# Message sums of a graph layer: rows stationary in 32 bit and a ring of sixteen slots, in a GNN and expert kernel on one core

## The reference

```python
def gcn_conv(x, W, b, src, dst, n_nodes):
    loop = jnp.arange(n_nodes)
    s = jnp.concatenate([src, loop])
    d = jnp.concatenate([dst, loop])
    ...
    norm = dinv[s] * dinv[d]
    xw = x @ W
    msg = xw[s] * norm[:, None]
    out = jax.ops.segment_sum(msg, d, num_segments=n_nodes)
    return out + b

out = gcn_conv(x, W1, b1, src, dst, N_NODES)
out = jax.nn.relu(batch_norm(out, gamma1, beta1))
out = gcn_conv(out, W2, b2, src, dst, N_NODES)
out = batch_norm(out, gamma2, beta2)
out = jax.nn.relu(out + identity)
```

## Time and profile before

| | us |
|---|---|
| median of three timed runs | 6407.3 |
| the profiled execution, its own time | 6353.42 |
| span of the profile | 6351.4 |
| TensorE busy in the span | 4421.4 (70%) |
| GpSimd busy | 3436.0 (54%) |
| VectorE busy | 1942.5 (31%) |
| ScalarE busy | 1190.9 (19%) |
| mean granted clock of TensorE | 0.709 |

### The profile page before, as it was taken

One profiled execution on the slowest core, in us unless ns is written; L12 is line 12 of the kernel. 1 busy time (PEld: TensorE's weight loads), 2 busy tenths in 40 slices (PEclk: granted clock), 3 DMA queues, 4 the chain that ended last, 5 costly groups with the idle time before them and its releaser, 6 DMA issues. The chain is left out here.

```text
span 6351.4 us, 77947 instructions
## 1 busy us (share of the span) xinstructions
PE 4421.4 (70%) x14346; PEld 2126.4 (33%) x14347; DVE 1942.5 (31%) x6975; ACT 1190.9 (19%) x2762; POOL 3436.0 (54%) x3661
## 2 busy tenths in 40 slices
PE   4567776676667766667766766666666665569999
PEld 3322222222222222232222222222222224448888
DVE  9411121211111112251122212212212216656665
ACT  5100000000000000020000000000000006635554
POOL 0266666666666666556666666666666662221111
PEclk5566666676666766766667676677677776679999
DMA  3643333333333333343333333333333332321111
GB/s 99 216 114 90 89 89 89 91 89 89 89 90 88 92 89 89 84 118 90 90 88 89 90 89 90 90 89 90 89 89 89 90 85 72 106 73 50 48 49 45
DMA packets 265568, 568.06 MB, mean 89 GB/s; under 512 B 67392, under 2 KB 139938, under 8 KB 265507
## 3 DMA queue, kind: packets, MB, share of 16 engines
q0 software_dynamic: 171264, 466.46, 25.5%
q1 hardware_dynamic: 94242, 100.94, 5.6%
HBM read 507.06 MB, written 60.09 MB: 89 GB/s over the span
## 5 line engine op out<-in xcount | busy, mean ns | idle before, releaser
L593 POOL DMA_INDIRECT ring<-messages,idx_stage x3328 | 3150.7, 947 | 1816.4 <-issue 875.5
L1591 PE MATMUL ps<-ring,onehot_mem 128*64 128x256 f32 x6656 | 2834.0, 547 | 1128.0 <-DMA ring<-messages,idx_stage 575.0
L1591 PEld LDWEIGHTS ps<-ring,onehot_mem 128*64 128x64 f32 x6656 | 933.4, 180 | 2665.9 <-DMA ring<-messages,idx_stage 1732.3
L1088 DVE TENSOR_TENSOR acc<-acc,ps 128x128 f32 x832 | 240.0, 288 | 3740.8 <-remote 2119.9
L727 ACT ACTIVATE win_rows<-ps 64x256 f32<-64x256 f32 x832 | 313.0, 377 | 2187.1 <-PE ps L1591 968.6
L1077 DVE TENSOR_SCALAR onehot_mem<-iota_bf,tables 128x64 f32<-128x64 bf16 x3344 | 647.4, 269 | 185.2 <-issue 135.8
L1488 PE MATMUL ps<-ident,win_rows 64*128 64x64 f32 x1664 | 340.0, 297 | 425.2 <-ACT win_rows L727 337.7
L1488 PEld LDWEIGHTS ps<-ident,win_rows 64*128 64x128 f32 x1664 | 207.9, 175 | 926.9 <-issue 926.9
L716 ACT ACTIVATE idx_stage<-tables 128x8 int32 (+1 forms) x420 | 87.0, 207 | 2292.0 <-PE ps L1591 982.5
L1796 PE MATMUL ps<-acc 128*128 128x256 f32 x2048 | 467.2, 380 | 0.8 <-ACT acc L890 0.8
L652 POOL DMA_INDIRECT out_dram<-acc x128 | 127.3, 995 | 600.7 <-DVE acc L1441 420.1
(11 more groups left out here) (250 smaller groups left out, 2213.4 us busy)
## 6 DMA issues: line engine op xcount, KB each, us to landing
ring<-messages,idx_stage POOLq DMA_INDIRECT x3328
rows_mem<-in_x_dram SPq DMA_DIRECT2D x62, 448.0 KB, 4.7
acc<-routed_rows SPq DMA_DIRECT2D x64, 264.0 KB
messages<-dinvT SPq DMA_DIRECT2D x28, 448.0 KB, 6.3
dinvT<-in_x_dram SPq DMA_DIRECT2D x22, 448.0 KB, 4.0
dinvT<-dinv_row SPq DMA_DIRECT2D x28, 224.0 KB
messages<-ring SPq DMA_DIRECT2D x14, 448.0 KB, 3.2
messages<-rows_mem SPq DMA_DIRECT2D x14, 448.0 KB, 3.2
```

Source lines behind the costliest of these rows:

```text
L593: pool.indirect_dma_start(out=slots[:, s, :], out_offset=None, in_=t_dram[layer], in_offset=bass.IndirectOffsetOnAxis(ap=idx_stage[:, u, s ...
L1088: dve.tensor_tensor(sums(w, WIN), sums(w, WIN), ps[:, 2 + u, 0:KH * WIN].rearrange("p (k w) -> p k w", k=KH), ALU.add).then_inc(ev_fast, 1)
L1591: pe.matmul(ps[0:WIN, u, 0:D], onehot[:, u, j, 0:WIN], slots[:, s, :], start=j == 0, stop=j == CPG - 1).then_inc(chunks_used, 1)
```

## The change

- The gathered rows, 32-bit, become the stationary operand. For each half k of the features and each chunk j, one matmul has 128 features of the slot stationary and moves the 64 columns of the one-hot. The group's sum appears as features by nodes in one bank, both halves side by side. Copy by ScalarE, turn by TensorE, `win_rows` and two semaphores go.
- VectorE adds straight from the bank. Four banks are used in turn, and four sets of one-hots (`DEEP` = 4), made four groups ahead.
- The ring has sixteen slots, eight in `ring` and eight in `rows_mem`. A group of four gathers counts up one semaphore (`got[q]`, 64 for a group), and TensorE waits once for all four.
- `chunks_used` is raised once a group, by four, on the last matmul. GpSimd waits for it once a group.
- The indices are still staged by eights (`STAGE`) in two buffers.

```diff
-SLOTS = 8
+SLOTS = 16
+DEEP = SLOTS // CPG
+STAGE = 8
...
-        slots = ring[:, 0:SLOTS * D].rearrange("p (s f) -> p s f", s=SLOTS)
-        onehot = onehot_mem[:, 0:2 * CPG * WIN].rearrange("p (u j w) -> p u j w", u=2, j=CPG)
+        slots = [mem[:, n * D:(n + 1) * D] for mem in (ring, rows_mem) for n in range(SLOTS // 2)]
+        onehot = onehot_mem[:, :].rearrange("p (u j w) -> p u j w", u=DEEP, j=CPG)
...
-                    for s in range(SLOTS):
-                        wait(pool, chunks_used, c0 + s - SLOTS + 1 + done)
+                    for h in range(STAGE // CPG):
+                        q = u * (STAGE // CPG) + h
+                        wait(pool, chunks_used, i * SLOTS + (q + 1) * CPG - SLOTS + done)
                         hold(pool)
-                        pool.indirect_dma_start(
-                            out=slots[:, s, :], out_offset=None, in_=t_dram[layer],
-                            in_offset=bass.IndirectOffsetOnAxis(ap=idx_stage[:, u, s:s + 1], axis=0),
-                        ).then_inc(got[s], 16)
+                        for j in range(CPG):
+                            n = h * CPG + j
+                            pool.indirect_dma_start(
+                                out=slots[q * CPG + j], out_offset=None, in_=t_dram[layer],
+                                in_offset=bass.IndirectOffsetOnAxis(ap=idx_stage[:, u, n:n + 1], axis=0),
+                            ).then_inc(got[q], 16)
...
-                    wait(act, chunks_used, (i - 1) * (2 * SLOTS) + u * SLOTS + SLOTS + done)
+                    wait(act, chunks_used, (i - 1) * SLOTS + (u + 1) * STAGE + done)
...
-                def keep_window(g, u):
-                    act.wait_ge(chunks_used, (g + 1) * CPG + done)
-                    wait(act, win_turned, g - 1 + layer * NG if not isinstance(g, int) or g > 1 else 0)
-                    hold(act)
-                    act.activation(win_rows[:, u, :], ps[0:WIN, u, 0:D], ACT.Copy).then_inc(win_kept, 1)
...
                 def fast(g, u):
                     dve.wait_ge(chunks_used, (g + 1) * CPG + run * GATHERS)
                     hold(dve)
-                    make_onehot(g + 2, u)
+                    make_onehot(g + DEEP, u)
                     w = dve.value_load(wrow[0:1, bass.ds(g, 1)], min_val=0, max_val=WMAX)
-                    dve.wait_ge(win_turned, g + 1 + run * NG)
...
-                def fast(i, q):
-                    g, u = i * 4 + q, q % 2
-                    pe.wait_ge(oh_fast, g + 1 + run * (NG + 2))
-                    for j in range(CPG):
-                        s = (q * CPG + j) % SLOTS
-                        landed(s, i * 2 + (q * CPG + j) // SLOTS)
-                        pe.matmul(ps[0:WIN, u, 0:D], onehot[:, u, j, 0:WIN], slots[:, s, :],
-                                  start=j == 0, stop=j == CPG - 1).then_inc(chunks_used, 1)
-                    if not isinstance(g, int) or g > 0:
-                        turn_window(g - 1, 1 - u)
+                def fast(i, q):
+                    g = i * DEEP + q
+                    pe.wait_ge(oh_fast, g + 1 + run * (NG + DEEP))
+                    wait(pe, ev_fast, g - DEEP + 1 + run * NG if not isinstance(g, int) or g >= DEEP else 0)
+                    landed(q, i)
+                    for k in range(KH):
+                        for j in range(CPG):
+                            last = pe.matmul(ps[:, q, k * WIN:(k + 1) * WIN], slots[q * CPG + j][:, k * P:(k + 1) * P],
+                                             onehot[:, q, j, :], start=j == 0, stop=j == CPG - 1)
+                    last.then_inc(chunks_used, CPG)
```

More of the change, by code:

```diff
@@ L127, in gnn_moe @@
         srcT = tables[:, TG * CPG:2 * TG * CPG]
-        ring = sb("ring", [P, max(SLOTS * D, 2 * BPC * (D + 8) + KH * CH)])
+        ring = sb("ring", [P, max(SLOTS // 2 * D, 2 * BPC * (D + 8) + KH * CH)])
         onehot_mem = sb("onehot_mem", [P, CPG * GWIN])
@@ L136, in gnn_moe @@
         iota_bf = sb("iota_bf", [P, GWIN], BF16)
-        idx_stage = sb("idx_stage", [P, 2, SLOTS], I32)
+        idx_stage = sb("idx_stage", [P, 2, STAGE], I32)
         relk = sb("relk", [P, CPG])
@@ L334, in gnn_moe @@
         GATHERS = NG * CPG
-        STAGES = GATHERS // SLOTS + 2
+        STAGES = GATHERS // STAGE + 2
         L1, L2 = 0, 1
@@ L721, in stages @@
                         stage(i, u)
-                def keep_window(g, u):
-                    act.wait_ge(chunks_used, (g + 1) * CPG + done)
-                    wait(act, win_turned, g - 1 + layer * NG if not isinstance(g, int) or g > 1 else 0)
-                    hold(act)
-                    act.activation(win_rows[:, u, :], ps[0:WIN, u, 0:D], ACT.Copy).then_inc(win_kept, 1)
                 def fours(i):
-                    for q in range(4):
-                        if q % 2:
-                            stage(i + 1, q // 2)
-                        keep_window(i * 4 + q, q % 2)
+                    stages(i + 1)
                 def add_bias(t):
@@ L933, in _ @@
             dve.tensor_copy(iota_bf[:, :], iota_i).then_inc(iota_bf_ready, 1)
-            dve.memset(ring[:, SLOTS * D:], 0.0)
+            dve.memset(ring[:, SLOTS // 2 * D:], 0.0)
             dve.wait_ge(edges_in, 32)
@@ L1131, in fours @@
                     for q in range(4):
-                        fast(i * 4 + q, q % 2)
+                        fast(i * DEEP + q, q)
                 def stride_end(g):
@@ L1140, in aggregate @@
                 with dve.If(bad == 0):
-                    for u in range(2):
+                    for u in range(DEEP):
                         make_onehot(u, u)
@@ L1569, in product @@
                     for k in range(KH):
-                        last = pe.matmul(ps[:, k, 0:GWIN], slots[:, s, k * P:(k + 1) * P], onehot_gen[:, j, :],
+                        last = pe.matmul(ps[:, k, 0:GWIN], slots[s][:, k * P:(k + 1) * P], onehot_gen[:, j, :],
                                          start=j == 0, stop=j == CPG - 1)
                     return last
-                def landed(s, use):
-                    pe.wait_ge(got[s], 16 * (use + done // SLOTS + 1))
-                def turn_window(g, u):
-                    pe.wait_ge(win_kept, g + 1 + run * NG)
-                    wait(pe, ev_fast, g - 1 + run * NG if not isinstance(g, int) or g > 1 else 0)
-                    hold(pe)
-                    for k in range(KH):
-                        last = turn(ps[:, 2 + u, k * WIN:(k + 1) * WIN], win_rows[:, u, k * P:(k + 1) * P])
-                    last.then_inc(win_turned, 1)
@@ L1585, in fast, with landed @@
[L1585 to L1594 removed]
+                def landed(q, use):
+                    pe.wait_ge(got[q], 16 * CPG * (use + done // SLOTS + 1))
@@ L1596, in general @@
                 def general(i, u):
-                    g = i * 2 + u
-                    for j in range(CPG):
-                        landed(u * CPG + j, i)
+                    g = i * DEEP + u
+                    landed(u, i)
                     hold(pe)
@@ L1630, in fours @@
                 def fours(i):
-                    for q in range(4):
+                    for q in range(DEEP):
                         fast(i, q)
@@ L1653, in aggregate @@
                 with pe.Else():
-                    with pe.Fori(0, NG // 2) as i:
-                        for u in range(2):
+                    with pe.Fori(0, NG // DEEP) as i:
+                        for u in range(DEEP):
                             general(i, u)
```

20 lines of the change are left out of this document (8 added, 12 removed).

## The result

The changed kernel takes 6489.06 us (median of 4 runs, 6484.09 to 6491.45) against 6406.89 us (6396.28 to 6411.36): ratio 1.013, 95% interval 1.0112 to 1.0147. It is 1.3% slower. The forecast was 5796 us in a range of 5680 to 6230: wrong in sign, and outside the range. The profiled run took 6484.09 us.

The account below looks back on a forecast made before the run. No engine was full; TensorE's late signals stalled GpSimd's gathers in the two aggregations. From 6353.4 us, minus 711 of stalls, plus 100 remaining, gives 5742; with 53.9 from profiled run to median, 5796 us, range 5680 to 6230.

Parts of the forecast that it names:

- The pace: Gathers in both aggregations: GpSimd starts one every 1.25 us by itself, so a layer takes 2079.7 us.
- TensorE's size: Products of a group: 16 records in 3.65 us slow or 1.9 fast, under the 5.0 us of four gathers.
- the fast cases: Remaining stalls with all products at the fast clock level: 178 us, weighted 0.36 against 410 us slow.
- VectorE locking GpSimd out: Rival in the aggregations: VectorE's 887 us of one-hots and sums hold up gathers, 6683 us; chance 0.03.
- The loop of the index copy: Index staging before every second group: 11.0 us slow, 9.25 fast, within 15.0, covering lateness of 4.0 or 5.75 us.
- What is left of the stalls: Aggregations: 832 measured latenesses played through the new waiting rules leave 326 us; cut to three quarters, 100 us.
- cover too short: Rival in the aggregations: lateness grows with what is queued; 6326 us, within 6022 to 6390; chance 0.12.
- the slower rival: Whole-group hand-over: steady lateness above 7.4 us makes the index loop longer than before; at 8.6, 6657 us; chance 0.10.
- 711 us of stalls: Both aggregations before the change: 353.8 + 357.5 us beyond GpSimd's own gather pace, all a deeper ring can bring.
- nothing left: Lower end of the forecast case: no stalls remain in the aggregations, 5696 us.
- the carried median: Whole kernel: the runs' median lies 53.9 us above the profiled run, added to the forecast.

Follow-up runs that it names:

- The run of 6333.68 us: The changed kernel with row numbers copied once the gathers reading the old ones have landed, not once TensorE used the rows; 6333.68 us, 0.9983 of the kernel before.
- by chunk: The changed kernel with TensorE waiting for and signalling each gather separately, and row numbers copied once their gathers landed; 6374.84 us, 1.004 of the kernel before.

## Why the prediction was wrong

- **The pace** held: 0.95 us busy and 0.30 idle, 1.25 from gather to gather, whatever surrounds it. A layer without stalls takes 2082.6 us where 2079.7 were worked out.
- **TensorE's size** held: 13312 records, waits for landings, 16 records in 3.65 us at the slow level and 1.90 at the fast one. The clock fell to 0.53, so it was at the slow level nearly throughout: 637 of 832 groups took 3.6 to 3.75 us and only 38 under 2.5, which took the fast cases out of the sum. One of those few:

```profile
1512.59 1.90 PE L1576 MATMUL ps<-onehot_mem,ring 128*128 128x64 f32 x16
```

- **VectorE locking GpSimd out** did not happen: 949 ns median with 3360 one-hots beside.
- **The loop of the index copy** was right in place: the stall sits before an even group, ended by the index copy. In size it was 0.5 us short. I had read 0.6 us from copy to gather off, where the gather at 1550.45 waited for a slot too ("remote"); behind a copy that is really waited for, the gather starts 1.06 us after it (middle half 1.05 to 1.07, 223 pauses), and as much in the run with signals 5.0 us late. So the loop is 11.5 us and covers 3.5, not 4.0, and 5.0 + 11.5 + 7.6 gives the 24.1 us of a round.
- **The step that failed is "What is left of the stalls".** I took 832 measured latenesses as a property of the signals, cut them to three quarters and played them through a longer cover: 100 us left. Measured: 854 us, 143 more than before. The run of 6333.68 us shows why: the lateness follows the cover. It is 7.7 us where 3.5 are covered and 12.7 to 14.2 where 9.8 are, and GpSimd pauses either way, the first signal coming 3.8 to 4.0 us after its last gather began. That the pause is what lets the signal go is argued from this timing; no run with a longer pause written in tested it. In the earlier trace rows the late signals did come together, after a long unbroken run of gathers. The "cover too short" rival said so and I gave it 0.12, and "it would have to be so always", with which I put off the slower rival, is exactly what a held signal does.
- **Why slower and not the same.** Where signals are late, the changed kernel and the one with the copy after landing both pause about once in 16 gathers whatever they cover (the one before once in 11, for less; by chunk once in 13). In the changed kernel the resuming gather also waits for ScalarE: signal 1542.78, copy 1542.93, gather 1543.99; and the product that has to end first is a whole group's. With the copy after landing the ratio is 0.9983 and not 1.013. That difference of 1.5%, some 95 us, is what the index copy costs where signals are late (compared through the kernel before, since the two ran on different chips); the rest of the change is worth 0.2% there.
- **The starting point.** 711 us of stalls are there in one measurement and not in another. On one without, the changed kernel takes 5593 us: the case "nothing left" had 5696, of which 54 us were the carried median and 54 are work outside the aggregations: 6351.4 - 4870.7 = 1480.7 us in the kernel before against 5591.6 - 4165.2 = 1426.4 in the changed kernel on chip 12. The changed kernel of the 6489 us has 6482.3 - 5013.4 = 1468.9 there, so most of it goes with the late signals, not with the change. Even the sign needs care: the kernel before is at 5600 us there, and the change gains nothing that can be told (0.999, 0.9978 to 1.0001).

Not settled: what holds TensorE's signals, and why a pause comes about once in 16 gathers. Nor is it shown that the chip decides: the measurements with late signals were the first and the last four (chips 7, 4, 4, 6), those without were the four between (12, 12, 0, 1), and no chip was seen both ways, so something that changed with time would look the same. That something between TensorE and the others fills up while GpSimd streams fits the products that come one at a time, but no run tested it. The obvious candidate is the profiler: every timed run here has a recorded span and clock, so each was profiled, and the semaphore updates go missing from the trace exactly where signals are late. Recording may hold TensorE, or both may have one cause; only a run without it could tell, and there is none. No version beat both kernels by more than 0.2%.

## What to carry to other kernels

A wait of unknown cause is not a random number to be covered; ask what ends it. Here its lateness ended with a pause of another engine, and more cover bought a longer lateness and the same pause. Before building on stalls that the profile can't name, run the unchanged kernel once more on a second chip and at another time, and look whether the trace has lost semaphore updates. Staged indices should be freed by what reads them (the landing), not by what uses the data.

## What was not expected of the hardware

- One program, two times: 5593 us and 6489 to 6496 us, 16% apart, each repeatable to 0.2% within its measurements, with the same median durations of gathers (949 and 947 ns) and product records (421 ns) and the same granted clock (0.53 and 0.54 in the aggregations).
- TensorE's signals seen up to 14 us after their product, with a DMA's signal on time beside them, and TensorE issuing one record in 0.7 or 1.4 us in the middle of a group that had landed.
- With that, two thirds of the semaphore updates missing from the trace (25115 of some 68700), at the same number of instruction records (78536).
- First release 3.8 to 4.0 us after the start of GpSimd's last gather where GpSimd waited for it; pauses of 3.6 us written in were too short in 99 of the 130 cases with a signal outstanding.
- The Trainium skill counts some 26 ns for each semaphore increment of TensorE's, where every tile's matmul makes one (TensorE: Matmul & The Clock Gate, "The cost: per-tile semaphore tail"). In the runs without late signals 0.23 us pass from a group's last product to VectorE's one-hot, all told (median, chip 12), which leaves room for it; in the others it is up to 14 us, which 26 ns a signal doesn't explain.
